# A two-layer graph network on one core: plain words sorted over four partitions, 34 of 50 tiles by one-hots, and the scatter of the next batch ahead of the gather

## The reference, cut to what matters

```python
h = relu(layernorm(x))
x = x + segment_sum((h * node_vec1)[src], dst) * node_vec1_n2          # layer 0
h = relu(layernorm(x))
m = relu(h[src] + edge_attr)
x = x + (1 + eps) * h + segment_sum(m, dst)                            # layer 1
```

## Time and profile before

| | us |
|---|---|
| median of 3 runs (4977.06 to 4985.43) | 4982.61 |
| span of the profiled execution | 8580.9 |
| busy in that span: TensorE | 4359.2 |
| busy: VectorE | 3658.4 |
| busy: GpSimd | 3610.0 |
| busy: ScalarE | 3124.7 |

### The profile page before, as it was taken

The page is one execution under the profiler, slowest core; times in us unless marked ns, Lnnn a source line. Parts: engine busy times, 40 slices in busy tenths (PEclk is TensorE's granted clock), DMA queues, the critical chain, the costliest instruction groups (busy, mean ns, idle before and its releaser), DMA issues.

```text
span 8580.9 us, 129759 instructions
## 1 busy us (share of the span) xinstructions
PE 4359.2 (51%) x44428; PEld 3164.9 (37%) x44428; DVE 3658.4 (43%) x11303; ACT 3124.7 (36%) x8299; POOL 3610.0 (42%) x3712
## 2 busy tenths in 40 slices
PE   0555555555555555555555555445444444545444
PEld 0333333333333333333333333334334343434343
DVE  6444444444444444444444444434343333434334
ACT  0333434343333333333333333234333333433333
POOL 7444444444444444444444444343443434343442
PEclk8777777777777777777777777666666666666666
DMA  5111111111111111111111100101110111101110
GB/s 90 31 31 31 31 31 31 31 30 31 30 31 30 31 30 31 30 31 30 31 30 31 31 17 17 43 22 31 30 32 22 32 29 32 31 22 32 30 32 17
DMA packets 437255, 265.45 MB, mean 31 GB/s; under 512 B 330740, under 2 KB 421220, under 8 KB 430120
## 3 DMA queue, kind: packets, MB, share of 16 engines
q1 hardware_dynamic: 318264, 185.91, 9.1%
q0 software_dynamic: 116960, 65.42, 4.4%
q10 hardware_dynamic: 1296, 4.79, 0.2%
HBM read 176.35 MB, written 79.52 MB: 30 GB/s over the span
## 4 chain that ended last, share of the span: by engine, by line
PE 36%; issue 26%; another core or an unknown queue 22%; DVE 9%; ACT 5%; SPq 1%; DVEq 0%; ACTq 0%; DMA 0%; POOL 0%; POOLq 0%
PE candidates L1179 16%; DVE arena L1663 5%; PE candidates L1105 5%; PE plain_ps L1191 4%; PE sorted_agg L1122 4%; DVE arena L1639 3%; PE key_rows L1074 2%; ACT centered L974 2%; PE candidates L1100 2%; ACT message L920 2%; PE plain_ps L1143 1%; PE candidates L1092 1%; ACT arena L821 1%; PE plain_ps L1151 1%
## 5 line engine op out<-in xcount | busy, mean ns | idle before, releaser
L710 POOL DMA_INDIRECT records<-stage,place_i x1875 | 1821.1, 971 | 675.8 <-issue 625.1
L698 POOL DMA_INDIRECT stage<-table,src_plain x1250 | 1193.9, 955 | 1778.1 <-DMA stage<-in_edge_attr 1386.7
L1639 DVE TENSOR_SCALAR arena<-arena,row_key 125x1280 bf16<-125x1280 f16 x1000 | 552.6, 553 | 2554.9 <-ACT arena L821 1776.0
L920 ACT ACTIVATE message<-candidates,member_is 128x96 bf16<-128x96 f32 x3600 | 912.4, 352 | 1643.5 <-remote 922.8
L691 POOL DMA_INDIRECT message<-table,mid_src x480 | 533.5, 1112 | 2234.8 <-PE plain_ps L1151 2095.5
L1105 PE MATMUL candidates<-parts,arena 125*128 125x32 bf16 x15000 | 589.2, 181 | 1214.2 <-issue 1211.8
L821 ACT ACTIVATE arena<-key_rows 125x640 f16<-125x640 f16 x1000 | 662.5, 719 | 1237.3 <-remote 987.2
L1663 DVE TENSOR_SCALAR arena<-window_iota,dst_rel 128x224 bf16<-128x224 f16 (+1 forms) x4800 | 1025.9, 280 | 112.4 <-remote 67.7
L1105 PEld LDWEIGHTS candidates<-parts,arena 125*128 125x128 bf16 x15000 | 503.7, 99 | 1384.6 <-issue 1370.1
L1092 PE MATMUL candidates<-parts,arena 125*128 125x96 bf16 x5000 | 312.0, 220 | 1312.9 <-ACT message L920 748.6
L1074 PE MATMUL key_rows<-ident,record 128*125 128x128 f16 x5000 | 494.6, 242 | 878.4 <-issue 587.7
(11 more groups left out here) (224 smaller groups left out, 5798.9 us busy)
## 6 DMA issues: line engine op xcount, KB each, us to landing
record<-records SPq DMA_DIRECT2D x50, 1650.0 KB, 7.1
stage<-in_edge_attr SPq DMA_DIRECT2D x125, 400.0 KB, 3.2
records<-pad SPq DMA_DIRECT2D x25, 1650.0 KB, 10.7
records<-stage,place_i POOLq DMA_INDIRECT x1875
stage<-table,src_plain POOLq DMA_INDIRECT x1250
message<-table,mid_src POOLq DMA_INDIRECT x480
xs<-in_x SPq DMA_DIRECT2D x8, 390.6 KB
table<-parts ACTq DMA_DIRECT2D x4, 585.9 KB
```

What stands on the lines that cost most here:

```text
L698: pool.indirect_dma_start(message[:, k, j, :] if l == 0 else rows[:, k, j, :], None, table0 if l == 0 else table1, bass.IndirectOffsetOnAx ...
L710: pool.indirect_dma_start(records, bass.IndirectOffsetOnAxis(ap=place_i[:, h, e:e + 1], axis=0), stage[:, h, e, :], None).then_inc(scatter ...
L920: last = nc.scalar.activation(direct_message[n % DB][:, m * WIDE:(m + 1) * WIDE], candidates[n % 2][:, m * WIDE:(m + 1) * WIDE], ACT.Copy, ...
L1639: nc.vector.tensor_scalar(src_onehot[:, g % 2, o, :], key_row[:, g % 2, :], row_key[0:NP, o:o + 1], None, ALU.is_equal).then_inc(src_oneho ...
```

## The change

- The plain words are sorted over four partitions together: they go to HBM once (`words`), two batches come back as 64 partitions x 200 words, VectorE sorts 200 words with 25 rounds of MAX8 and MATCH_REPLACE8 (`sort_pair`), the result goes to HBM (`ordered`) and comes back as 128 x 2 x 50 words (`row_words`), which `read_words` splits. The rounds are spread over steps 2 to 6 of two successive batches.
- A tile now meets fewer groups (`SPANS`, 3 to 8 in its first 17 entries), 17 tiles at either end go by one-hots, and 16 are gathered. The 34 tiles go through eight steps; `FIRST[3]` is tile 13.
- GpSimd's program scatters batch b + 1 before it gathers batch b.
- The scans take one operand from PSUM (`goes_on`), in slices of 20 buckets instead of 25, and the prefix is added from PSUM; ScalarE's copy of it is gone.
- The SyncE queue moves the words of a pair, and waits for the end of the sort for it; ScalarE's queue does so once at the start.

The diff, cut to its core:

```diff
-    BOUNDS = (6, 7, 8, 8, 9, 9, 10, 10, 11, 11, 12, 12, 13, 13, 14)
-    SIDE = len(BOUNDS)
+    SPANS = ((0, 3), (0, 3), (0, 4), (0, 5), (0, 5), (0, 6), (0, 6), (0, 7), (1, 7), (1, 8),
+             (1, 8), (1, 9), (2, 9), (2, 10), (2, 10), (3, 10), (3, 11), (3, 11), (4, 12), (4, 12))
+    SIDE = 17
...
+    CUTS = (0, 5, 9, 13, 17)
+    SIDE_STEPS = len(CUTS) - 1
+    SUBS = 2 * SIDE_STEPS
+    ROOMS = [("far", "arena", "near")[k % 3] for k in range(SUBS - 2)] + ["far", "near"]
+    STEPS = [(LOW, range(CUTS[k], CUTS[k + 1]), ROOMS[k]) for k in range(SIDE_STEPS)]
+    STEPS += [(HIGH, range(CUTS[k + 1] - 1, CUTS[k] - 1, -1), ROOMS[2 * SIDE_STEPS - 1 - k]) for k in reversed(range(SIDE_STEPS))]
...
+        SCANNED = 20
+        goes_on = sorted_agg[1][:, 0:SCANNED * J]
...
+                if is_first(b):
+                    load_pair(2, u)
+                if sorts_ahead(b) and h == 1:
+                    load_pair(b + 3, u + 1)
+                if sorts_ahead(b) and h == 0:
+                    sp.wait_ge(pair_steps, PAIR_STEPS * (u + 1))
+                    sp.sem_inc(loads_begun, 1)
+                    sp.dma_start(ordered_rows[bass.ds((b + 2) * QUADS, 2 * QUADS), :], pair_left).then_inc(words_out, 16)
+                    sp.wait_ge(words_out, 16 * (u + 3))
+                    sp.sem_inc(loads_begun, 1)
+                    sp.dma_start(row_words, ordered_v[:, bass.ds(b + 2, 2), :]).then_inc(words_loaded, 16)
...
             def step0(b, h, u):
-                scatter(b, h, u)
+                if not is_last(b):
+                    scatter(*after(b, h, u))
...
                     if not is_first(b):
                         pool.wait_ge(plain_done[0], b)
                     gather_mid(h)
+            scatter(0, 0, 1)
             over_batches(pool, step0)
...
-            def copy_prefix(b):
-                act.wait_ge(prefix_ready, b + 1)
-                nc.scalar.activation(prefix16[:], prefix, ACT.Copy).then_inc(prefix_copied, 1)
...
+                if l == 0:
+                    act.wait_ge(direct_keyed, 1)
+                    act.dma_start(words_v[:, 0:BATCHES, :], row_order[:]).then_inc(words_out, 16)
...
+                    act.dma_start(pair_left, words_rows[0:2 * QUADS, :]).then_inc(pair_loaded, 16)
+                    act.wait_ge(pair_steps, PAIR_STEPS)
+                    act.dma_start(ordered_rows[0:2 * QUADS, :], pair_left).then_inc(words_out, 16)
+                    act.wait_ge(words_out, 48)
+                    act.dma_start(row_words, ordered_v[:, 0:2, :]).then_inc(words_loaded, 16)
...
-                            if n == FIRST[4] and left_after(b) >= 2:
+                            if n == FIRST[SUBS - 2] and left_after(b) >= 2:
                                 prefixes(b + 2)
...
-                        last = nc.vector.tensor_tensor_scan(counts[:, v, some], not_first[:].rearrange("p g j -> p (g j)")[:, some],
+                        last = nc.vector.tensor_tensor_scan(counts[:, v, some], goes_on[:, 0:some.stop - some.start],
                                                             in_bucket[:, v, some], 0.0, ALU.mult, ALU.add)
...
-                        prefix16[:, v * BUCKETS:(v + 1) * BUCKETS].unsqueeze(2).to_broadcast([P, BUCKETS, J]), ALU.add))
+                        prefix[:, v * BUCKETS:(v + 1) * BUCKETS].unsqueeze(2).to_broadcast([P, BUCKETS, J]), ALU.add))
...
+            def sort_pair(u, some):
...
+                for r in some:
+                    eight = pair_best[:, 8 * r:8 * r + 8]
+                    dve.sem_inc(rounds_begun, 1)
+                    step(nc.vector.max(out=eight, in_=pair_left))
+                    if r < ROUNDS8 - 1:
+                        dve.sem_inc(rounds_begun, 1)
+                        step(nc.vector.match_replace(out=pair_left, in_to_replace=eight, in_values=pair_left, imm_value=-1.0))
...
+                HALF_ROUNDS = ROUNDS8 // 2
+                SORTED_IN = range(2, SUBS - 1)
...
-                            sort_rows(b + 1, 1 - h)
...
+                        for s in range(SUBS):
+                            wide_onehots(b, s)
+                            if s == 1 and more:
+                                dve.wait_ge(words_loaded, 16 * (u + h))
+                                read_words(b + 1, 1 - h)
+                            if s == 2:
+                                add_sorted(b)
+                            sort_some(b, h, u, s)
+                            direct_onehots(b, h, s)
+                            if s == SUBS - 3 and more:
+                                rank_within(b + 2, h, u + 1)
                         if more:
                             rank_sums(b + 2)
                             rank_places(b + 2, h, u + 1)
```

More of the change, by code:

```diff
@@ L80, in gnn_two_layers @@
     MID = PJ - DIRECTS
-    STEPS = ((LOW, range(4, -1, -1), "far"), (LOW, range(14, 9, -1), "arena"), (LOW, range(9, 4, -1), "near"),
-             (HIGH, range(14, 9, -1), "arena"), (HIGH, range(4, -1, -1), "far"), (HIGH, range(9, 4, -1), "near"))
-    SUBS = len(STEPS)
     SUB = 5
+    CUTS = (0, 5, 9, 13, 17)
[4 more added lines that the diff above has]
+    STEPS += [(HIGH, range(CUTS[k + 1] - 1, CUTS[k] - 1, -1), ROOMS[2 * SIDE_STEPS - 1 - k]) for k in reversed(range(SIDE_STEPS))]
+    LAST_ARENA = max(k for k in range(SUBS) if ROOMS[k] == "arena")
     TILE_OF = [(side, r) for side, ranks, _ in STEPS for r in ranks]
@@ L101, in met_by @@
     def met_by(side, r):
-        return range(BOUNDS[r]) if side == LOW else range(WIDES - BOUNDS[r], WIDES)
-    STEP_GROUPS = [met_by(side, ranks[0]) for side, ranks, _ in STEPS]
+        least, beyond = SPANS[r]
+        return range(least, beyond) if side == LOW else range(WIDES - beyond, WIDES - least)
+    STEP_GROUPS = [range(met_by(side, ranks[0]).start, met_by(side, ranks[-1]).stop) for side, ranks, _ in STEPS]
+    SHARED = 4
+    WIDTH = SHARED * PJ
+    QUADS = P // SHARED
+    FLAGGED = 2.0 ** 23
     PAIRS_BY = [sum((len(c) + 1) // PAIR for c in STEP_GROUPS[0:k]) for k in range(SUBS + 1)]
@@ L262, in gnn_two_layers @@
         wide_rooms += [record[0:NP, 1, :, :].rearrange("p t w -> p (t w)").bitcast(BF16)[:, w * SE5:(w + 1) * SE5] for w in range(IN_X)]
-        NEAR = BOUNDS[9]
-        assert NEAR + BOUNDS[4] <= len(wide_rooms)
+        NEAR = IN_X
+        assert all(len(STEP_GROUPS[k]) <= IN_X for k in range(SUBS) if ROOMS[k] != "arena")
         def wide_onehot(k, w):
@@ L288, in gnn_two_layers @@
         dst_far = sb("dst_far", [P, J], I32)
-        far = sb("far", [P, J])
-        far_dst = sb("far_dst", [P, J])
-        far_key = sb("far_key", [P, J])
+        far, far_dst, far_key = (row_room[:, (6 + k) * P:(6 + k) * P + J] for k in range(3))
         BANK = 512
@@ L680, in _ @@
                       allow_small_or_imprecise_dtypes=True).then_inc(consts_ready, 1)
-            for r in range(SIDE):
-                pool.memset(bound[:, LOW, SIDE - 1 - r:SIDE - r], float(BOUNDS[r] * P)).then_inc(bounds_ready, 1)
-                pool.memset(bound[:, HIGH, r:r + 1], float((WIDES - BOUNDS[r]) * P)).then_inc(bounds_ready, 1)
+            GROUP_WORDS = P * LOWER
+            for q in range(PJ):
+                groups = met_by(HIGH, q) if q < SIDE else met_by(LOW, PJ - 1 - q) if q >= PJ - SIDE else range(WIDES)
+                pool.memset(least_word[:, q:q + 1], float(groups.start * GROUP_WORDS)).then_inc(bounds_ready, 1)
+                pool.memset(beyond_word[:, q:q + 1], float(groups.stop * GROUP_WORDS)).then_inc(bounds_ready, 1)
             pool.iota(members[:], pattern=[[1, MEMBERS]], base=0, channel_multiplier=0,
@@ L1356, in node_rows @@
                         table_parts(l, k)
-            RANK1 = 9 + 2 + 5
+            SCANS = [slice(g * J, min(g + SCANNED, BUCKETS) * J) for g in range(0, BUCKETS, SCANNED)]
+            RANK1 = 8 + SORTED + SORTED * len(SCANS) - 1
             def rank_within(b, h, u):
@@ L1764, in first_onehots, with rounds_in, sort_some @@
                         dst_onehots(b, h, u, g)
+                HALF_ROUNDS = ROUNDS8 // 2
+                SORTED_IN = range(2, SUBS - 1)
+                def rounds_in(s, begun, ended):
+                    nth, n = s - SORTED_IN.start, len(SORTED_IN)
+                    return range(begun + nth * (ended - begun) // n, begun + (nth + 1) * (ended - begun) // n)
+                def sort_some(b, h, u, s):
+                    if not sorts_ahead(b) or s not in SORTED_IN:
+                        return
+                    if h == 1:
+                        sort_pair(u + 1, rounds_in(s, 0, HALF_ROUNDS))
+                    else:
+                        sort_pair(u, rounds_in(s, 0 if is_first(b) else HALF_ROUNDS, ROUNDS8))
                 def step0(b, h, u):
```

156 lines of the change are left out of this document (85 added, 71 removed).

## The result

The changed kernel takes 5908.67 us (median of 4 runs, 5900.12 to 5912.22) against 4982.05: a ratio of 1.186 (95% interval 1.184 to 1.188). The forecast was 5820, 5350 to 6100. The profiled execution of the changed kernel is not stretched as that of before was: its span, 5905.3 us, is that of the runs.

What follows compares the result with a forecast made beforehand. It took TensorE and GpSimd as both about full. 23 periods of 163 instead of 128 us (+805), start +29 and end +5, added to 4982.6, gave about 5820 us, range 5350 to 6100.

Steps and rivals of the forecast that it cites:

- The loop: Once a batch: mid_products(b), ranks of b + 2, 75 scatters, 16 gathers, mid_products(b + 1); 163 us, chance 0.79.
- Legs 1, 2 and 4: Loop parts: mid_products until direct one-hot 24 is free, 6 us; VectorE to the ranks' end, 40; 16 gathers, 20.
- Leg 3: Loop part on GpSimd: 75 scatters at 1.27 us each, VectorE idle for part of it, 95 us.
- the landing: Loop's last part, landing of the last gather before mid_products: not visible in the trace, put at 2 us.
- the period before: Time per layer 0 batch in the kernel before: between 119 and 132 us, taken as 128.
- SyncE's queue: Waits for the sort, so TensorE's records land 0 to 10 us late every second batch; counted as nothing.
- GpSimd's relief: On GpSimd, 16 gathers a batch instead of 20: 5 us less of its demand.
- The faster rival: Scatter and gathers fit before mid_products, the loop is slack, period 117 us, total 4720 us; chance 0.12.
- p: Price of one indirect DMA on GpSimd; the loop is 48 + 91 p, equal to 128 at 0.88 us.
- Leg 1: Loop part on TensorE: mid_products(b) and tile 14 until direct one-hot 24 is free; 4 at full clock, put at 6 us.
- leg 2: Loop part on VectorE: direct one-hot, rank_within, steps 6 and 7, rank_sums and rank_places; 40 us.

Runs made afterwards that it cites:

- e1: The changed kernel with the old order on GpSimd (scatter batch b, then gather batch b): 4839.98 us, ratio 0.970.
- e2: The kernel before with only GpSimd's order changed, scatter of batch b + 1 ahead of the gathers of batch b: 5741.72 us, ratio 1.152.
- e9: The changed kernel, with SyncE writing the padding of batch b + 2 as soon as the scatter of batch b has begun: 5887.79 us, ratio 1.181.
- e5: e1 with 15 tiles at either end by one-hots instead of 17, and 20 gathered: 4958.29 us.
- e7: e1 with 19 tiles at either end by one-hots instead of 17, and 12 gathered: 4879.48 us.
- e6: e1 with 20 tiles at either end by one-hots instead of 17, and 10 gathered: 4908.93 us.
- e11: e1 with 18 tiles at either end by one-hots instead of 17, and 14 gathered: 4874.44 us.
- e4: e1 with the scans as before, both operands in SBUF, six slices of 25 buckets; the prefix still added from PSUM: 4857.98 us.
- e3: The changed kernel, its order on GpSimd kept, with mid_products moved from tile 13 to the last tile (33): 4915.04 us, ratio 0.986.
- e8: The changed kernel with its sort rounds in steps 2 to 5 of a batch instead of 2 to 6: 5908.30 us, ratio 1.185.

## Why the prediction was right

**The loop, leg by leg.** It is there, and it is the cause: undone in the changed kernel it gives back 1069 us (e1), put into the kernel before it costs 754 (e2). Legs 1, 2 and 4 came as worked out: 6.0 us where 6 was put, 40.4 for 40, 19.7 for 20. Leg 3 was 95.4 to 97.0 for 95, and the landing 1.5 and 5.0 in turn for 2. Together 165.9 us instead of 163. The bounds put beside the sum, 156 to 186, are not those of its legs, which add up to 158.5 and 192; 165.9 lies within both.

**Where the 89 us above 5820 come from.** 23 x 2.9 = 67 from the period; 1 from the start (first `mid_products` at 263.3, 262 forecast); the other 20 lie behind the last `mid_products`, 1829 us where the sum had 1809, since it took the period before a little too long (below). The means of the 23 turns split the 2.9: 1.4 are the scatters (96.4 us for 95, so 1.29 each and not 1.27), 1.2 the landing (3.2 for 2), 0.6 the way from `mid_products` to the first scatter (46.6 for 46, with 1.0 between the ranks and the scatter that no leg held), and the gathers give 0.3 back. So two terms were a little small. The landing I had set near nothing because a gather moves 25 KB, and had counted SyncE's queue for TensorE alone; e9 shows that its padding delays the last gather by 3.5 us in every second turn.

**The period before.** I took 128 us. e2 bounds it: its layer 1 and end take 5741.7 - 3918.3 = 1823 us; if before has the same, and its first `mid_products` lies at 233 (my sum) to 254 (as in e1), its period was (4982 - 1823 - 233 or 254) / 23 = 126 to 127. So the stretched trace still gave a usable period from its undisturbed stretches. The one matmul in 2.8 us beside the scatters is not seen again: in e1 GpSimd issues all the time, and TensorE is busy for 1889.5 of 2300 us (600 to 2900).

**GpSimd's relief.** The faster rival needed p below 0.88 us. The changed kernel's own scatters go at 96.5 / 75 = 1.29 from start to start, e1's at 1.30. The relief itself is real and shows as soon as the order is undone: e1 is faster than before by 148 us, and giving the four gathers back (e5) takes 118 of them away, 4.9 us a batch.

**TensorE's clock.** Leg 1 allowed for a lower clock after a wait. The windows show it: granted 0.52 in 1712 to 1764 us, while TensorE stands, 0.50 in the four us after a wait, near the 1.2 GHz level, and 0.97 in the next 40; `mid_products` takes 3.22 us there and 1.70 in e1, at 1.00.

**VectorE.** MAX8 and MATCH_REPLACE8 on 200 words take 0.360 and 0.343 us (0.37 and 0.35 put), a round 1.09; the scans took 9.50 for 8.94 and 0.8 more forecast. The prefix adds take 1.455 us from PSUM against 1.5 before, so the lower tier that the Trainium skill gives an operand in PSUM (VectorE: DVE Perf Modes, "The perf-mode tier table") cost nothing here: the adds already took 1.2 ns an element. What I had wrong is the sentence that VectorE "stays below the others" at 99 us: in e1 it is busy for 1968.2 of 2300 us, 102 a period, and with the short gaps between its instructions it is nearly as full as GpSimd. In the changed kernel, where it waits some 44 us a batch, that cost nothing beyond leg 2; it is why more tiles do not help e1 (shown in e7's window; for e6 and e11 it is argued from their times and gaps).

**SyncE's wait for the sort.** TensorE waited 11 times for late records, 3.0 us each (110.1 us in 12 waits, less 76.6 at the start), beside the longer waits, as counted. It did matter in another way: it kept SyncE's traffic away from every second batch's gathers.

**The scans from PSUM.** The Trainium skill (SBUF — State Buffer, "Who interferes with whom") says that a Vector instruction with two SBUF inputs contends with a GpSimd one that reads SBUF, and that one with a single SBUF input, outside the two-port modes, does not. e4 agrees: mostly 1.19 us against 0.96 for a scatter, 18 us in all.

## What to carry to other kernels

When two jobs on one queue change places, write down the whole ring of waits that the new order closes, through every engine, with the number of periods that it spans: a ring of 166 us within one period cost 19%, one of 244 us over two periods (e3) 2 us a period. A consumer placed late in an in-order program holds everything behind it, so moving it out of one ring makes a longer one, not none. A saved part (four gathers, 5 us a batch) is worth its sum only while the engine that it relieves sets the period; here the best of the kernels keeps all of the change but the order, 4839.98 us.

## What was not expected of the hardware

The landing of the last gather depended on one transfer of a direct queue: 1.4 to 1.7 us with SyncE's padding out of the way (e9), 4.7 to 5.9 with those 1650 KB under way (e8). A gather that ran beside VectorE's multiply of 3750 elements, both inputs in SBUF, took 2.42 us in place of 0.94 (e1), more than any scatter beside the scans.
